# Turning x for two of four chunks with VectorE's block transpose and block-placing loads, in a Mamba-2 scan with an MLP

## The reference, cut to what matters

```python
x = layernorm(x + attn(x))          # the scan below, then an MLP
x = layernorm(x + ffn(x))

def mamba2(xn, ...):
    zxbcdt = xn @ w_in              # z, x|B|C, dt
    xc = silu(conv4(x|B|C) + conv_b)
    xh, Bm, Cm = split(xc)          # 512, 128 and 128 channels
    dt = softplus(dt_raw + dt_bias)
    u = dt[..., None] * xh          # tokens x channels
    # in chunks: y_diag from C, B, the decays and u; states from B, decays, u; y_off from C and the states
    y = y_diag + y_off + d_skip[:, None] * xh
    g = rmsnorm(y * silu(z)) * norm_w
    return g @ w_out
```

## Time and profile before

| what | value |
|---|---|
| median of 3 runs | 1225.0 us (1224.75 to 1227.83) |
| the profiled execution | 1225.03 us, its span 1223.3 us |
| TensorE matmul busy | 1196.1 us (98%) |
| VectorE busy | 783.3 us (64%) |
| ScalarE busy | 645.9 us (53%) |
| GpSimd busy | 232.4 us (19%) |
| SyncE's DMA queue | 71.51 MB, 18.0% of 16 engines' span |

### The profile page before, as it was taken

One profiled execution on the slowest core, in us unless ns is written; L12 is line 12 of the kernel. 1 busy time (PEld: TensorE's weight loads), 2 busy tenths in 40 slices (PEclk: granted clock), 3 DMA queues, 4 the chain that ended last, 5 costly groups with the idle time before them and its releaser, 6 DMA issues.

```text
span 1223.3 us, 19219 instructions
## 1 busy us (share of the span) xinstructions
PE 1196.1 (98%) x6468; PEld 1007.1 (82%) x6468; DVE 783.3 (64%) x1363; ACT 645.9 (53%) x1213; POOL 232.4 (19%) x210
## 2 busy tenths in 40 slices
PE   8899999999999999999999999999999999999996
PEld 6678888888888888788888888888888888888885
DVE  6798898989899898855535337345363363543633
ACT  6788888878788888666224124142141331422420
POOL 0517153534434261610000000000000000000000
PEclk9999999999999999999999999999999999999998
DMA  8222211222222221134500202002002020020000
GB/s 284 82 82 75 83 70 51 63 88 75 96 75 97 75 73 64 66 128 172 212 1 1 52 1 51 0 0 51 0 6 45 0 51 0 0 51 0 18 1 18
DMA packets 60696, 72.05 MB, mean 59 GB/s; under 512 B 33520, under 2 KB 52080, under 8 KB 58736
## 3 DMA queue, kind: packets, MB, share of 16 engines
q1 hardware_dynamic: 60656, 71.51, 18.0%
HBM read 63.10 MB, written 22.03 MB: 70 GB/s over the span
## 4 chain that ended last, share of the span: by engine, by line
issue 53%; POOL 0%; DVE 0%; POOLq 0%; DVEq 0%
POOL rsv_b L1885 0%; DVE o_sb L1962 0%; POOLq L1883 0%; DVEq L1716 0%; POOL rsv L235 0%; POOLq L442 0%
## 5 line engine op out<-in xcount | busy, mean ns | idle before, releaser
L1869 ACT ACTIVATE full<-bank,scale 128x512 f32<-128x512 f32 x128 | 88.3, 690 | 383.1 <-PE bank L1778 383.1
L1778 PE MATMUL bank<-hB_hi,h_sb 128*128 128x512 f32 x512 | 199.9, 390 | 0.0
L1778 PE MATMUL bank<-hB_lo,h_sb 128*128 128x512 f32 x512 | 199.7, 390 | 0.0
L1778 PE MATMUL bank<-hA_hi,h_sb 128*128 128x512 f32 x512 | 199.6, 390 | 0.0
L1778 PE MATMUL bank<-hA_lo,h_sb 128*128 128x512 f32 x512 | 199.5, 390 | 0.0
L1931 DVE CAST hA_hi<-full 128x512 fp32r<-128x512 f32 x64 | 27.4, 427 | 173.1 <-ACT full L1869 173.1
L1885 POOL TENSOR_TENSOR rsv_b<-mv_b,eps 128x4 f32<-128x4 f32 x8 | 10.7, 1342 | 618.2 <-DVE mv_b L187 618.2
L1778 PEld LDWEIGHTS bank<-hA_lo,h_sb 128*128 128x128 f32 x512 | 96.1, 188 | 20.2 <-DMA h_sb<-ffn_raw 0.2
L1778 PEld LDWEIGHTS bank<-hA_hi,h_sb 128*128 128x128 f32 x512 | 96.2, 188 | 20.0
L1778 PEld LDWEIGHTS bank<-hB_hi,h_sb 128*128 128x128 f32 x512 | 96.4, 188 | 19.1
L1778 PEld LDWEIGHTS bank<-hB_lo,h_sb 128*128 128x128 f32 x512 | 96.3, 188 | 18.9
(11 more groups left out here) (230 smaller groups left out, 2982.1 us busy)
## 6 DMA issues: line engine op xcount, KB each, us to landing
chk_xh<-w_ffn SPq DMA_DIRECT2D x16, 704.0 KB, 4.1
ffn_raw<-w_ffn SPq DMA_DIRECT2D x8, 1408.0 KB, 6.8
h_sb<-ffn_raw SPq DMA_DIRECT2D x2, 4096.0 KB, 19.4
xT<-x_t SPq DMA_DIRECT2D x8, 512.0 KB, 6.2
x_res<-x SPq DMA_DIRECT2D x8, 512.0 KB, 3.7
x_rows<-x SPq DMA_DIRECT2D x8, 512.0 KB, 3.3
x_in<-x_rows SPq DMA_DIRECT2D x8, 512.0 KB, 5.1
x_in<-x SPq DMA_DIRECT2D x7, 512.0 KB, 4.7
```

The source lines that it names most:

```text
L1778: ins = pe.matmul(o, a_, b_, start=first and n == 0, stop=last and n == 1, skip_group_check=True)
L1869: nc.scalar.activation(full[:, n % FULL, :], b[:], ACT.Gelu, scale=scale[:, 1 + n // KH, n % KH:n % KH + 1]).then_inc(s_gd, 1)
```

## The change

In tiles 1 to 7 the x blocks of chunks 2 and 3 are turned another way; tile 0 and chunks 0 and 1 stay as they are. VectorE transposes the 32x32 squares of xc's columns for both chunks in one operation, `turn_squares`, into two blocks of xp (2 and 5) that are free at that time. SyncE stores these to DRAM, waits for the landing, and loads them per chunk with four loads, each to 32 partitions, which put the squares at their places in xt. TensorE's eight transposes and ScalarE's two copies in a tile go, with their places in the order of bank items. GpSimd waits for the loads instead of the copies. ScalarE waits for the store before it writes xp's blocks 2 and 5 again.

The places: `turn_squares` stands between VectorE's masks of chunk 0 and of chunk 1; the store and the loads of chunk 2 stand ahead of xT of the next tile in SyncE's order, the loads of chunk 3 behind spread_rstd.

```diff
     order += ["fc3", "fc4", "fc5"] * mlp
-    order += ["xt2", "gb2", "xt3"]
+    order += ["gb2"] if mlp else ["xt2", "gb2", "xt3"]
...
+        sq_dram = nc.dram_tensor("x_squares", (P, KI * len(LATE) * P), F32, kind="Internal").ap()
...
+        squares = xp[:, 2::3, HALO:]
+        SQUARE_LOADS = 16 * (P // SQ)
...
+                def store_squares(i, loaded, stored):
+                    sp.wait_ge(s_sq, i)
+                    for s_l in s_late:
+                        ge(sp, s_l, loaded)
+                    sp.dma_start(sq_dram.rearrange("p (g n) -> p g n", g=2), squares).then_inc(s_sqs, 16)
+                    sp.wait_ge(s_sqs, stored)
+
+                def load_turned(n, s_free, count):
+
+                    c = LATE[n]
+                    sp.wait_ge(s_free, count)
+                    src = sq_dram.rearrange("(j a) (m c q b) -> c q a m j b", a=SQ, m=KI, c=len(LATE), b=SQ)
+                    for q in range(P // SQ):
+                        dst = xt[q * SQ:(q + 1) * SQ, c % 2, :].rearrange("a (m j b) -> a m j b", m=KI, b=SQ)
+                        sp.dma_start(dst, src[n][q]).then_inc(s_late[n], 16)
+
                 def tile(i, at, at_x, at_xT, at_out, piece, half, next_half):
+                    kept = lambda v: v if isinstance(v, int) else sp.snap(v)
+                    loaded, stored = kept(SQUARE_LOADS * (i - 1)), kept(16 * i)
+                    u_made, skip_made = kept(CH * i + 1), kept(CH * i + 2)
+                    store_squares(i, loaded, stored)
+                    load_turned(0, s_u, u_made)
                     if at_xT is not None:
                         load_xT(i + 1, at_xT)
                         spread_rstd(i + 1)
+                    load_turned(1, s_skip, skip_made)
+                    if at_xT is not None:
                         sp.wait_ge(s_rsl, 16 * i + 16)
                     load_residual(i, at)
...
                     y_off(w, i, 1)
-                    turn_x(w, i, 2)
+                    if not mlp:
+                        turn_x(w, i, 2)
...
-                    turn_x(w, i, 3)
+                    if not mlp:
+                        turn_x(w, i, 3)
...
+                    if m in (2, 5):
+                        ge(act, s_sqs, 16 * (t - 1))
...
-                    rows(w, i, 2)
+                    if not mlp:
+                        rows(w, i, 2)
...
-                    rows(w, i, 3)
+                    if not mlp:
+                        rows(w, i, 3)
...
+                def turned_x(w, i, c):
+                    if c in LATE and w is not w_first:
+                        pool.wait_ge(s_late[LATE.index(c)], SQUARE_LOADS * i)
+                    else:
+                        pool.wait_ge(s_ad, w.act(f"xt{c}") + 1 + ACT_BANKS)
+
                 def make_u(w, i, c):
-                    pool.wait_ge(s_ad, w.act(f"xt{c}") + 1 + ACT_BANKS)
+                    turned_x(w, i, c)
...
                 def make_skip(w, i, c):
-                    pool.wait_ge(s_ad, w.act(f"xt{c}") + 1 + ACT_BANKS)
+                    turned_x(w, i, c)
...
+                def turn_squares(t):
+                    dve.wait_ge(s_halo, t + 1)
+                    dve.wait_ge(s_xc, MC * t + MC - 1)
+                    nc.vector.transpose(squares.rearrange("p g (m n) -> p g m n", m=2),
+                                        xc[:, 0:KI, LATE[0] * P:].rearrange("p (g m) n -> p g m n", g=2)).then_inc(s_sq, 1)
...
                     mask_exponents(w, 0)
+                    if mlp:
+                        turn_squares(i)
                     mask_exponents(w, 1)
```

More of the change, by code:

```diff
@@ L137, in post_ln_block @@
     PIECE = FFN_WORDS // TILES
+    SQ = 32
+    LATE = (2, 3)
     HALVES = 2
@@ L379, in post_ln_block @@
         flat3 = lambda ap: ap[:].rearrange("p k n -> p (k n)")
+        s_sq = sem("x_squares_turned")
+        s_sqs = sem("x_squares_stored")
+        s_late = [sem(f"turned_x_of_chunk_{c}_loaded") for c in LATE]
         s_x = sem("x_loaded")
@@ L1679, in post_ln_block @@
         x1_in, x1_res = x_in, sb("x1_res", [P, CH, D])
-        SQ = 32
         BLOCK_LOADS = 16 * KD * (P // SQ)
```

## The result

The changed kernel takes 1241.96 us in the median of four runs (1240.43 to 1243.47), the kernel before 1225.14 us beside it (1224.75 to 1227.83): a ratio of 1.013, 95% interval 1.0114 to 1.0147, or +16.8 us. The forecast was 1231 us, +6. The direction was right and the upper end of the range (1242) holds it by 0.04 us, but the size is off by a factor of nearly three.

A forecast was written before the change was run, and what follows sets the result against it. TensorE was taken to bound the kernel, with VectorE close behind. Tiles 1 to 6 at +1.0 us each and tile 7 at +0.1 gave +6 us on 1225, so 1231 us, with a range of 1221 to 1242.

The forecast's parts named there:

- TensorE's saving of 0.72 us in a tile: TensorE loses two groups of four transposes per tile, 0.36 us each; 5.0 us over seven tiles.
- rival (1): x_rstd in time and VectorE's delay swallowed, so TensorE's saving stays: -5.0 us, 1220 us; chance 0.12.
- The transpose: VectorE's block transpose between the masks of chunks 0 and 1: 1.24 us of work, not held by GpSimd.
- y_diag: TensorE's y_diag of chunk 0 waits for VectorE's later scores: +0.8 us in each of tiles 2 to 7.
- SyncE's issues: In SyncE's queue the store is issued at 299.25 and the x_rstd row at 305.8 instead of 304.94.
- The row's landing: The x_rstd row, behind xT and block loads on SyncE, takes 2.8 us to land; x_rstd arrives at 312.5.
- rival (3): Queue decides: row lands only with xT's 6.2 us; +3.7 us in six tiles, 1247 us; chance 0.17.
- From x_rstd to xbc1: From VectorE's norm_x at 312.5 to TensorE's xbc1 at 317.2 or 317.3: +0.7 us on the tile.
- GpSimd's hold of 0.3 us on the way: GpSimd's u of chunk 3 and following ud move over VectorE's adds and xnT_lo, holding them 0.3 us.
- Chunks 2 and 3 arrived in time: Loaded x for GpSimd: chunk 2 lands near 308, needed 310.65; chunk 3 near 314, its u formerly at 316.0.
- (2) the draw: Queue hidden, only the transpose counts: 0.1 to 0.3 us per tile, 1224 to 1227 us; chance 0.23.
- its halved form: Half the late-queue loss, if the x_rstd row lands at 310: 1238 to 1243 us; within rival (3)'s 0.17.

The follow-up runs named there:

- e7: Kernel before plus only SyncE's store and eight loads, started after the second masks, loads unused, x still turned by TensorE: 1231.91 us, ratio 1.0049.
- e8: Changed kernel without VectorE's transpose; store and loads stay, TensorE's groups stay away, x of chunks 2 and 3 is wrong data: 1233.32 us, ratio 1.0067.
- e9: Changed kernel with TensorE's transposes of chunks 2 and 3 put back; VectorE's transpose, store and loads stay, loads unused: 1236.32 us, ratio 1.0086.
- e1: Changed kernel with SyncE issuing xT, store, x_rstd row and spread first, then awaiting the store's landing and issuing all eight loads: 1227.39 us, ratio 1.0011.
- e4: Kernel before with only VectorE's block transpose added in tiles 1 to 7, no store or loads, squares unused: 1228.76 us, ratio 1.0023.
- e5: Changed kernel with the queue order of e1 and VectorE's transpose moved behind the sum of x_res and h: 1226.08 us, ratio 1.0002.
- e3: Changed kernel with six extra unread 128x128 products on TensorE between chunk 3's two exponents in tiles 1 to 6: 1234.06 us, ratio 1.0063.
- e2: Changed kernel with only the next tile's xT moved ahead of the store; the row stays behind chunk 2's loads: 1229.39 us, ratio 1.0025.

## Why the prediction was right or wrong, point by point

Two terms of the sum failed: the landing of the x_rstd row was taken as 2.8 us and measured 3.5, and the clock behind TensorE's new idle time was put at nothing and cost 5 to 8 us. The other steps follow in the order of the working.

- **TensorE's saving of 0.72 us in a tile: wrong as a saving.** The instructions went, the time didn't. The sum for a tile used it only to say when TensorE would arrive at xbc1 (316.64), and there it was rightly covered by x_rstd; but tile 7, tile 1 and rival (1) took it at full. e7 with e8, and e9 with the changed kernel, put it at zero or below; e1 with e4 leave 0.2 us a tile beside the store and the loads.
- **The transpose: right.** Priced at 1.24 us from the earlier trace rows, measured 1.23; the strided output cost nothing that the row shows. y_diag: predicted +0.8 us, measured +0.6 (5.44 us after the first masks instead of 4.82), since yoff starts at 300.18 where I had 300.3 and the scores take 1.20 us instead of 1.35. e4 gives +2.7 us for it alone; that is 0.6 for each middle tile, less in tile 1, as said. It was not held by GpSimd.
- **SyncE's issues: right to 0.1 us.** The store was forecast at 299.25 and issued at 299.25, the row at 305.8 and came at 305.88.
- **The row's landing: the term that was mis-sized.** 2.8 us taken, "nearest to the 2.5", and 3.5 measured; the spread took 4.1, not 3.9. x_rstd thus lands at 313.3 and not 312.5. The mechanism that decides was that of rival (3), which I gave 0.17: the row lands only with xT. In this tile xT, issued 0.51 us ahead, took 3.6 us to landing (315.96), and the row 3.5 (316.36). I had priced this with xT's 6.2 us of before; at its new place xT's median is 4.0. The sum also went against the rule that I cited for it: with xT issued at 305.3 and 6.2 us to landing, the row could not have landed at 308.6. The row's four values (1.4 alone, 2.0 behind the block loads, 2.2 behind a store issued 1.1 us ahead, in e5, 3.5 behind xT) follow what stands right ahead. The Trainium skill (DMA: Bandwidth & Descriptors, Queues, rings and completion order) says that a completion increment lands only after every earlier write of that DMA engine. The trace agrees: in no tile of any run did the row land before a transfer issued ahead of it. The rule should have been given more weight than the nearest row.
- **From x_rstd to xbc1: right.** With 3.5 and 4.1 us put in, my own working gives norm_x at 313.3 to 313.5 and the second exponents some 1.5 us later than before; tile 5, at full clock, is 1.6 us longer. So the period at full clock should have been forecast as 68.3 instead of 67.7: over six tiles +9.6 us instead of +6. At full clock +8.6 came, since tile 1 grew by only 0.3 us (67.8 to 68.1 between its first masks and those of tile 2) where I had +1.0.
- **GpSimd's hold of 0.3 us on the way: wrong.** From norm_x to the start of xnT_lo it is 323.47 - 320.32 = 3.15 us, shorter than the 3.45 of before. Chunks 2 and 3 arrived in time, as forecast.
- **The clock: absent from the sum.** Up to 6.6 us by the tiles' lengths, 4.7 and 7.9 us by e3. This is the largest single miss, and the sum had no term for it: I priced a wait of TensorE at its length. In tile 4 the clock read 0.50 in three windows of 1 us, and what ran there needed about 1.2 us longer. The Trainium skill (TensorE: Matmul & The Clock Gate, HAM oscillation) describes a kernel in which waits for DMAs put the clock down anew in every round. The trace agrees, in four of six tiles, and with idle times under 2 us.
- **Does it add up?** 8.6 (x_rstd and y_diag at full clock) + 6.6 (clock) = 15.2 of the 15.4 us between the two profiles. The medians are 16.8 apart: the changed kernel's other three executions are 1.4 to 3.0 us slower than the profiled one, at mean clocks of 0.989 to 0.991 against 0.992, and have no profile. Against the forecast's +6, the row's landing and the spread are the smaller part of the miss (2.6 us) and the clock the larger. e4's +2.7 and e7's +5.9 are 8.6 too; e9, with both, measured +10.5. The 1.9 us between lie within the intervals. A part of them may be the store, which stands behind the transpose and so starts about 0.8 us later in the tile (2.60 us after the first masks in e9, 1.77 in e7): norm_x's wait for x_rstd is 1.0 us longer in all. This was not isolated.

Rivals: (1) everything hidden and (2) the draw fell to the wait for x_rstd; e1 is what (2) would have been, 1227.4 against "1224 to 1227". (3) had the mechanism and a price too high in its full form; its halved form, 1238 to 1243, had the time, but by luck, since 6.6 us of that are the clock. That the range held 1241.96 is luck for the same reason: its upper end stood for a late row, and without the falls of the clock the time comes to some 1234 us, an estimate (1225.1 + 8.6).

## What to carry to other kernels

Before adding transfers to a queue, find the smallest DMA in it whose landing somebody waits for, and take its landing as no earlier than the last landing among the transfers in flight ahead of it; moving that one issue (e2) or the small one (e1) was worth 13 to 15 us here. Work removed from the bounding engine paid nothing here while its next input came late; it can pay only if the engine's next input comes earlier too: look at the wait behind the removed work first. And give a new idle time of TensorE a price above its length, as a chance and not as a certainty: here 1.3 to 1.9 us of it came with a tile about 1.6 us longer than one at full clock in four tiles of the changed kernel, and without in one, and the same kernel differs from execution to execution.

## What the runs showed of the hardware that I had not expected

- In tiles 1 to 6, TensorE's granted clock fell to the 1.2 GHz level behind single idle times of 1.29 to 1.85 us in otherwise full work and stayed there for about 3 us; behind idle times up to 1.02 us it did not fall there. Between 1.29 and 1.68 us both were seen. Filling the idle time with 1.5 us of unread products made the whole kernel 7.9 us faster in the median.
- These lengths are no threshold: in tile 0 the clock fell in e7 behind 0.46 us (16.9 us), in five of eleven profiles in all, and in the kernel before it did not fall behind 2.04 us (until 7.96). With two such falls y_diag of tile 0 starts at 43.15 to 43.93 us, in the six profiles without any at 40.09 to 41.59.
- A 2 KB store took 1.4 us to landing alone and 3.5 us right behind a 512 KB load on the same queue, which it never overtook.
- A 512 KB load of the same shape took 6.2 us in one place of the queue and 4.0 in another: a landing time read in one place is no bound for another.
